# Two-layer graph transformer: GpSimd fills a 128x300 two-byte tile in front of each gather of rows

## The reference, cut to what matters

```python
h = relu(layernorm(x))                       # x: 6250 x 128, float32
for l in range(2):                           # two layers, 8 heads of 16, 8 node types, 8 relations
    k, q, v = (typed_linear(h, ntype, W[l]) for W in (Wk, Wq, Wv))
    a   = (rel_apply(k[src], etype, Watt[l]) * q[dst]).sum(-1) * pri[l][:, etype].T / 4.0
    ex  = exp(a - segment_max(a, dst)[dst])  # 100000 edges, sorted by dst
    alpha = ex / (segment_sum(ex, dst)[dst] + 1e-16)
    agg = segment_sum(alpha[..., None] * rel_apply(v[src], etype, Wmsg[l]), dst)
    o   = silu(typed_linear(agg, ntype, Wa[l]))
    al  = sigmoid(skip[l][ntype])[:, None]
    h   = layernorm(o * al + h * (1 - al)) * g[l] + b[l]
return x + h @ Wff + bff
```

## Time and profile before

| what | value |
|---|---|
| time, median of 3 runs | 2810.78 us (2806.79 to 2811.38) |
| span of the profiled execution, core 0 | 3418.8 us |
| the profiled execution's own time | none is listed beside its span |
| mean granted TensorE clock in it | 0.698 |
| busy share PE, DVE, ACT, POOL | 61%, 63%, 45%, 57% |
| gathers of the edge stages (L1242) | 1564, mean 945 ns |

### The profile page before, as it was taken

One profiled execution on the slowest core, in us unless ns is written; L12 is line 12 of the kernel. 1 busy time (PEld: TensorE's weight loads), 2 busy tenths in 40 slices (PEclk: granted clock), 3 DMA queues, 4 the chain that ended last, 5 costly groups with the idle time before them and its releaser, 6 DMA issues. The chain is left out here.

```text
span 3418.8 us, 52858 instructions
## 1 busy us (share of the span) xinstructions
PE 2097.2 (61%) x12592; PEld 1812.6 (53%) x12592; DVE 2154.3 (63%) x5522; ACT 1534.9 (45%) x5149; POOL 1947.8 (57%) x2030
## 2 busy tenths in 40 slices
PE   2567726666666666666566626666666666666565
PEld 1455515556566555655444525556655555555544
DVE  6576527666666666666555626666666666666577
ACT  0015514444444444544555614444444444444554
POOL 4415555666666666666355564666666666666265
PEclk6568867776767777677677866776777767777655
DMA  5416655555555555555245554555555555555321
GB/s 125 80 74 262 274 159 143 152 154 157 154 153 153 154 155 151 156 154 152 71 188 200 218 161 141 148 153 155 152 155 155 154 157 156 153 153 151 111 56 31
DMA packets 386069, 511.26 MB, mean 150 GB/s; under 512 B 75321, under 2 KB 298235, under 8 KB 373268
## 3 DMA queue, kind: packets, MB, share of 16 engines
q0 software_dynamic: 101952, 326.75, 30.8%
q1 hardware_dynamic: 274712, 179.39, 17.9%
q10 hardware_dynamic: 9104, 1.86, 0.3%
HBM read 382.63 MB, written 142.96 MB: 154 GB/s over the span
## 5 line engine op out<-in xcount | busy, mean ns | idle before, releaser
L1242 POOL DMA_INDIRECT g_rows<-node_kv,edge_key_sb x1564 | 1478.4, 945 | 913.1 <-issue 415.8
L1412 ACT ACTIVATE acc<-g_ps_sum 128x127 f32 x1564 | 420.5, 269 | 691.9 <-issue 498.9
L1477 PE MATMUL g_ps_sum<-g_hot,g_rows 128*128 128x128 f32 x3128 | 597.1, 348 | 163.5 <-ACT acc L1416 118.0
L1496 PE MATMUL g_ps_q<-g_qw,g_hot_t 128*128 128x128 f32 x3128 | 629.6, 372 | 106.7 <-DVE g_rows L1268 43.5
L1416 ACT ACTIVATE acc<-acc,g_gained,g_scale x1564 | 601.1, 384 | 136.0 <-issue 120.5
L1477 PEld LDWEIGHTS g_ps_sum<-g_hot,g_rows 128*128 128x128 f32 x3128 | 545.1, 259 | 203.7 <-ACT acc L1416 138.2
L1496 PEld LDWEIGHTS g_ps_q<-g_qw,g_hot_t 128*128 128x128 f32 x3128 | 586.6, 282 | 119.5 <-issue 58.0
L1522 PE MATMUL g_ps_a<-g_ends,head_of_row 112*8 112x56 f32 x224 | 38.0, 270 | 551.9 <-DVE g_alpha L1303 461.9
L1485 PE MATMUL g_ps_hot<-ident,g_hot_t 128*128 128x128 f32 x1564 | 310.9, 325 | 50.6 <-issue 29.0
L1268 DVE TENSOR_TENSOR g_rows<-g_rows,g_ps_q 128x512 f32<-128x512 f32 (+1 forms) x446 | 263.3, 608 | 118.2 <-remote 85.2
L1522 PEld LDWEIGHTS g_ps_a<-g_ends,head_of_row 112*8 112x8 f32 x224 | 13.5, 88 | 576.1 <-issue 576.1
(11 more groups left out here) (247 smaller groups left out, 3204.1 us busy)
## 6 DMA issues: line engine op xcount, KB each, us to landing
g_qw<-node_q SPq DMA_DIRECT2D x1564, 64.0 KB
g_rank_row<-edge_rank SPq DMA_DIRECT2D x110, 448.0 KB
g_rows<-node_kv,edge_key_sb POOLq DMA_INDIRECT x1564
node_agg<-n_agg SPq DMA_DIRECT2D x24, 256.0 KB, 2.3
node_rows<-node_x SPq DMA_DIRECT2D x2, 1792.0 KB
node_q<-l_blank_q SPq DMA_DIRECT2D x1, 3200.0 KB
node_q<-n_q_sb,node_slot POOLq DMA_INDIRECT x112
node_kv<-n_kv,node_id POOLq DMA_INDIRECT x112
```

Source lines behind the costliest of these rows:

```text
L1242: g_.indirect_dma_start(out=rows[b % U][:, g, :], out_offset=None, in_=scratch["kv"][:, :], in_offset=bass.IndirectOffsetOnAxis(ap=tab["ke ...
L1412: a.activation(acc[:, bass.ds(w + 1, P - 1)], ps_sum[q % 2][:, n, 1:P], ACT.Copy).then_inc(s["copied"], 1)
L1477: ins = t.matmul(ps_sum[q % 2][:, n, :], rows[b % U][:, g, D:2 * D], hot[b % U][:, g, :], start=True, stop=True)
L1496: ins = t.matmul(ps_q[q % 2][:, n, :], hot_t[b % 2][:, g, :], qw[b % 2][:, g, :], start=True, stop=True)
```

## The change

In `edge_stage` one more tile in SBUF, `idle`, of 128 partitions by 300 two-byte elements, and in POOL's list a fill of it with zeros in front of every gather. Each fill adds one to a new semaphore `idle`; each but the first waits until the fill before it is counted, and the list ends with a wait for all 782. Nothing reads the tile.

```diff
         whole = sb("whole", [H, G])
+        idle = sb("idle", [P, 300], BF16)
         seam = sb("seam", [GH, P + 1], BF16)
...
                         if g % FOUR == 0 and b >= U:
                             pool.wait_ge(s["sums"], GROUP[b - U] + g // FOUR + 1)
                         at = FIRST[b] + g
+                        if at > 0:
+                            pool.wait_ge(s["idle"], at)
+                        g_.memset(idle[:, :], 0.0).then_inc(s["idle"], 1)
                         g_.indirect_dma_start(out=rows[b % U][:, g, :], out_offset=None, in_=scratch["kv"][:, :],
                                               in_offset=bass.IndirectOffsetOnAxis(ap=tab["key"][:, at:at + 1], axis=0)).then_inc(rows_in[2 * (b % U) + (g >= EARLY)], 16)
 
                 over(batch, 0)
+                pool.wait_ge(s["idle"], EDGE_TILES)
```

## The result

The changed kernel takes 3172.61 us (3172.11 to 3173.86), beside 2811.08 us for the kernel before: a ratio of 1.1291, with a 95% interval of 1.1278 to 1.1305. That is 361.5 us more, or 0.231 us for each of the 1564 gathers. The forecast was 3296 us, with a range of 3090 to 3520.

What follows compares the result with a forecast made beforehand. POOL was taken to bound the timed edge stages at 1.25 us a gather, 17.5 us a batch. Each fill adds 0.31 us in full: 1564 x 0.31 = 485 us on 2810.8 gives 3296 us, range 3090 to 3520.

Steps and rivals of the forecast that it cites:

- POOL sets the pace of the timed runs with 17.5 us a batch: Edge stages: 14 gathers at 1.25 us fill POOL's batch without slack; DVE, PE and ACT need 1 us or more less.
- The stops: Edge-stage waits where several engines resume together about 3 to 4 us late; said to belong largely to the profiled execution.
- A fill of 300 two-byte elements has a row of 347 ns and keeps POOL for 0.31 us: Added fill on POOL: 0.833 ns an element, elements counting rather than bytes; 0.31 us taken, 0.35 as upper end.
- It comes on top of the 1.25 us in full: Between two POOL gathers: nothing of the fill hides, 0.31 us for each of 1564 gathers, 485 us in all.
- the rival of the hidden fill: Fill hides in the 0.30 us before each gather: 2826 us, half hidden 3061, or no change; chance 0.09.
- The forecast's own branch: POOL pays 0.31 to 0.35 us per gather in full: 3250 to 3380 us; chance 0.62.
- half the elements: POOL's fill issued as four-byte words, 150 elements, 0.19 us each: 3108 us; chance 0.04.
- an engine other than POOL: Edge stages: another engine set the timed pace at 18.7 us a batch, POOL had slack: 3163 us; chance 0.10.
- Going from fill to gather costs 0.25 us more: Rival on POOL: up to 0.25 us extra per gather after a fill, 391 us more, 3687 us; chance 0.15.
- The waits for the fill before cost nothing: POOL's wait before each fill: the earlier fill is over, covered by the gather in between; cost nothing.
- Other engines lie 1 us or more beneath POOL: Edge-stage batch: DVE's step put at 15.0 to 16.5 us, with PE and ACT also under POOL's 17.5.
- The span should grow by 99 us at least: Changed kernel's profile: batch from 20.96 to 21.84 us, span 3517 us at least; 485 us growth if stops stay.

## Why the prediction was right, and where its size was off

1. *POOL sets the pace of the timed runs with 17.5 us a batch, though the trace of before shows 21 with slack on POOL.* Right, and shown: 17.52 us from batch to batch in the trace that fits the time, 1.25 us a gather, and DVE waits for rows. The arithmetic that led there (the time that 1955 us of gathers leave for the rest) gave at most 856 us for what lies outside the gathers. The two traces have it: 2808 - 1955 = 853, and 3171 - 1564 x 1.48 = 856. It is POOL's instructions and not the transfers that set the pace: the fills move no bytes (511.39 MB against 511.26), and yet the two stages grow from 978.2 and 976.6 us to 1160.8 and 1159.6, first gather to last.
2. *The stops belong largely to the profiled execution.* Wrong as worded. They came back in the traces of three jobs in which every run of the kernel before took 3344 to 3389 us. What was right is only that the 2811 us didn't have them. On which chip the first trace was taken is not on record.
3. *A fill of 300 two-byte elements has a row of 347 ns and keeps POOL for 0.31 us.* The row measured 365 ns. Elements count, not bytes: right.
4. *It comes on top of the 1.25 us in full.* This is the term that was mis-sized: 0.23 instead of 0.31 us, 361.5 instead of 485. It was the rival of the hidden fill in part, at 0.23 us between its 0.16 and the full 0.31. The 0.30 us in front of a gather runs from the end of the gather before, and a fill runs inside it. What shows in the rows is: next gather at 0.30 us after the last one's end, or at about 0.165 us after the fill's end, whichever is later. With 300 elements: 0.95 + 0.365 + 0.165 = 1.48. With 150: 0.95 + 0.24 + 0.165 = 1.355. With 2: 0.95 + 0.30, and the few ns that the gather's own row is longer (medians 952 against 946). These sums are fitted to the rows and were not forecast; a second trace of the 150 elements has 1.356 again. What the 0.30 us is spent on, no row tells. So 0.135 us of each fill is free, and the cost of 300 elements is 0.365 - 0.135 = 0.23; 1564 x 0.23 = 360. The prediction leaned on the one row of a fill before a gather, whose 0.56 us said that nothing is hidden. That was the program's first gather and stood for no other.
   That the range held is in part luck. The forecast's own branch, 3250 to 3380, missed. The range reached down to 3090 only for two rivals, half the elements (3108) and an engine other than POOL (3163), and the runs refute both; 3163 lies nearest to the result for a wrong reason. The rival that was right in part, the hidden fill, was the one that the range left out.
5. *Going from fill to gather costs 0.25 us more.* No: the gather's row went from 946 to 952 ns (medians), and the gap before it shrank from 0.30 to 0.17 us.
6. *The waits for the fill before cost nothing.* Right: 0.003 us each at most, by the spacings of the 24-element fills, and in the changed kernel no fill waited.
7. *Other engines lie 1 us or more beneath POOL.* Close: the next limit is 16.55 us, 0.97 under 17.52. It isn't DVE's own work but its wait for ACT's flags, which the prediction's sum of busy times had no term for.
8. *The span should grow by 99 us at least.* It fell by 248, since the first trace of before had the stops and the changed kernel's has none. Forecasting a difference of spans from a trace whose span didn't fit the time was a mistake; the time forecast stood on the median.

The Trainium skill, "Perfetto Trace Analysis", section "GPSIMD Engine Instruction", tells to go by the spacing of starts on this engine. The trace agrees: summing rows (0.955 + 0.365 = 1.32 us) is 0.16 short of the 1.48 that a pair takes, and adding the fill's row to the old spacing (1.25 + 0.365 = 1.615) is 0.135 too much.

## What to carry to other kernels

When a trace's span is far from the timed runs, ask first which engine has a fixed need that fits the shorter time; here 14 gathers x 1.25 us was the timed batch, and the 3.5 us of slack that POOL had in the long trace did not exist in the short one. Then get a trace whose span fits. Even there POOL's busy share is only 70% while it never stops in the edge stages, because a fixed 0.30 us of every gather counts as idle; start-to-start spacing shows it. A small instruction put between such instructions is partly free, here about 0.135 us of it: a fill of 0.12 us cost 0.007, one of 0.24 us 0.106, one of 0.365 us 0.23.

## What the runs showed that I had not expected

- The kernel before has two levels, by job: 2809 to 2811 us and 3379 to 3383. At the 3380 level every part but the last is a fifth to a quarter longer (361 against 438 us up to the first gather of edges, 977 against 1180 for an edge stage, 278 against 349 for the node stage between), though single rows of POOL and DVE are not: a gather has 945 and 946 ns, DVE's L1353 2.00 us at both. It is the waits that grow, and SP's issues show it plainly: 0.54 us for each window of queries on average against 0.91. Fourteen windows, timeline of SP in the two traces of the kernel before, first the 2810 and then the 3380 level:

```profile
1015.47 7.14 SPq L1223 DMA_DIRECT2D g_qw<-node_q  x14
```

```profile
1011.89 13.06 SPq L1223 DMA_DIRECT2D g_qw<-node_q  x14
```

- At the 3380 level the edge stages have the same length whatever POOL does up to 1.356 us a gather (1179 to 1186 us with fills of 0, 2, 24 and 150 elements), yet leaving out one gather of 14 gives 129 us and two 202. So something that hangs on the gathers, but not on POOL's time for them, sets the pace there. Which it is, why it differs from job to job, and what the change costs at that level stay open; none of these runs tells.
